# Gathers of a graph layer on GpSimd: a wait per gather for its own row buffer, and gather indices copied two tiles earlier

## What is computed

```python
def layer(h, params):
    W, b, g, beta = params
    h = h * norm_out
    agg = jax.ops.segment_sum(h[src], dst, num_segments=n)
    agg = agg * norm_in
    out = agg @ W + b
    out = _layer_norm(out, g, beta)
    out = jax.nn.gelu(out, approximate=False)
    return (out, None)
h, _ = jax.lax.scan(layer, features, (Ws, bs, ln_g, ln_b))
...
x = _layernorm(x + h)
```

## Time and profile before

| what | value |
|---|---|
| median of three runs | 1668.79 us (1665.58 to 1670.16) |
| profiled execution, its own time | 1669.91 us |
| its span, first to last instruction | 1668.2 us |
| mean granted TensorE clock | 0.808 of full speed |
| busy share of the span | TensorE 67%, weight loads 55%, DVE 53%, GpSimd 51%, ACT 32% |
| DMA | 224.52 MB moved, 135 GB/s |

### The profile page before, as it was taken

One profiled execution on the slowest core, in us unless ns is written; L12 is line 12 of the kernel. 1 busy time (PEld: TensorE's weight loads), 2 busy tenths in 40 slices (PEclk: granted clock), 3 DMA queues, 4 the chain that ended last, 5 costly groups with the idle time before them and its releaser, 6 DMA issues.

```text
span 1668.2 us, 29286 instructions
## 1 busy us (share of the span) xinstructions
PE 1110.4 (67%) x6235; PEld 916.9 (55%) x6235; DVE 880.2 (53%) x2153; ACT 528.1 (32%) x853; POOL 846.9 (51%) x1023
## 2 busy tenths in 40 slices
PE   7665378677596695776776696679956769992000
PEld 7444123666575575656656585667846667882000
DVE  6445577245354372463563274326733226776776
ACT  4132230232332332233333232333323333441444
POOL 1554300545445464455455365445745445765886
PEclk9556559788898897798898898789987889996555
DMA  0930000523514415225225324441244448545998
GB/s 14 377 130 3 2 1 6 159 82 126 158 57 139 133 69 170 78 107 163 71 106 164 107 76 138 139 126 66 91 139 147 149 126 321 189 169 180 312 302 291
DMA packets 98038, 224.52 MB, mean 135 GB/s; under 512 B 14496, under 2 KB 14496, under 8 KB 97968
## 3 DMA queue, kind: packets, MB, share of 16 engines
q0 software_dynamic: 34432, 104.72, 21.2%
q1 hardware_dynamic: 57200, 107.52, 17.9%
q10 hardware_dynamic: 6336, 11.54, 1.9%
HBM read 137.91 MB, written 85.82 MB: 134 GB/s over the span
## 4 chain that ended last, share of the span: by engine, by line
PE 53%; issue 12%; DMA 10%; DVE 8%; POOL 5%; ACT 4%; another core or an unknown queue 3%; ACTq 2%; DVEq 2%; POOLq 0%; SPq 0%
PE ps_a L1200 16%; PE ps_y L1220 9%; PE ps_y L1221 9%; PE ps_y L1225 9%; DMA rows<-h_rows,slot 4%; POOL rows L507 3%; DMA rows<-h_rows,idx_f 2%; PE ps_y L1216 2%; DMA h_rows<-rows 2%; PE ps_a L1115 2%; DVE agg_t L607 2%; PE ps_a L1181 1%; ACT agg_t L958 1%; DVEq L821 1%
## 5 line engine op out<-in xcount | busy, mean ns | idle before, releaser
L1200 PE MATMUL ps_a<-sel,rows 128*128 128x128 f32 x2560 | 407.0, 323 | 278.1 <-DVE sel L789 122.8
L1200 PEld LDWEIGHTS ps_a<-sel,rows 128*128 128x128 f32 x2560 | 377.1, 233 | 309.6 <-issue 309.0
L456 POOL DMA_INDIRECT rows<-h_rows,slot x290 | 279.8, 965 | 258.3 <-issue 124.6
L995 ACT ACTIVATE agg_t<-ps_a 128x508 f32 x320 | 190.7, 596 | 520.7 <-PE ps_a L1200 369.8
L464 POOL TENSOR_TENSOR s_lo<-agg_t,s_hi 128x512 fp32r<-128x512 f32 x168 | 216.9, 1293 | 251.3 <-ACT s_hi L1000 251.3
L789 DVE TENSOR_SCALAR sel<-iota,by_tile 128x128 f32<-128x128 f32 x344 | 126.0, 370 | 395.6 <-PE ps_a L1200 207.2
L1220 PE MATMUL ps_y<-w_hi,s_hi 128*128 128x512 f32 x672 | 268.5, 400 | 10.9 <-ACT s_hi L1000 10.8
L1221 PE MATMUL ps_y<-w_lo,s_hi 128*128 128x512 f32 x672 | 267.6, 398 | 0.0
L1225 PE MATMUL ps_y<-w_hi,s_lo 128*128 128x512 f32 x672 | 183.5, 396 | 0.0
L862 DVE BATCH_NORM_STATS2 small<-ps_y 128x6 f32<-128x512 f32 x168 | 117.3, 698 | 96.1 <-PE ps_y L1225 95.9
L1220 PEld LDWEIGHTS ps_y<-w_hi,s_hi 128*128 128x128 f32 x672 | 129.0, 192 | 42.0 <-issue 15.1
(11 more groups left out here) (210 smaller groups left out, 1268.2 us busy)
## 6 DMA issues: line engine op xcount, KB each, us to landing
h_rows<-rows SPq DMA_DIRECT2D x124, 256.0 KB, 2.0
h_rows<-agg_t SPq DMA_DIRECT2D x1, 20480.0 KB
out<-agg_t SPq DMA_DIRECT2D x78, 256.0 KB
agg_t<-in_x SPq DMA_DIRECT2D x19, 1024.0 KB, 5.7
h_rows<-rows ACTq DMA_DIRECT2D x44, 256.0 KB, 2.3
w_raw<-in_Ws SPq DMA_DIRECT2D x32, 256.0 KB
rows<-h_rows,slot POOLq DMA_INDIRECT x290
rows<-in_ln_g SPq DMA_DIRECT2D x8, 256.0 KB, 3.8
```

The source lines that it names most:

```text
L456: g.indirect_dma_start(out=rows[:, k, :], out_offset=None, in_=table[:, :], in_offset=bass.IndirectOffsetOnAxis(ap=slot[:, k:k + 1], axis=0))\
L995: a.activation(agg_t[:, :, bass.ds(r0 + 1, P - 1)], ps_a[k % GS][:, :, 1:P], ACT.Copy)\
L1200: m = mm(ps_a[k % GS][:, b, :], rows[:, k, b * P:(b + 1) * P], sel[:, k % GS, :], start=True, stop=True)
```

## The change

GpSimd now waits before every gather, for the tile that used this very row buffer ten tiles before. DVE copies a half's next indices at its third tile (k = 2 and 7) instead of its fifth (k = 4 and 9), and before that waits until the half's last gather of this group (k = 4 and 9) has landed, since this gather reads `slot` too. PRIME goes from 8 to 10, because the new wait reaches nine tiles back.

```diff
-PRIME = 8
+PRIME = 10
...
                         if k % GS == 0:
                             pool.wait_ge(ix_ok, ib * 2 + group * 2 + (L * 2 + k // GS + 1))
                             pool.sem_inc(tick, 1)
-                            pool.wait_ge(agg_ok, done(i + k - GS))
-                            pool.sem_inc(tick, 1)
+                        pool.wait_ge(agg_ok, done(i + k - UN + 1))
+                        pool.sem_inc(tick, 1)
                         g.indirect_dma_start(out=rows[:, k, :], out_offset=None, in_=table[:, :],
...
                             v.tensor_tensor(col, ps_a[k % GS][:, :, 0:1], col, ALU.add).then_inc(edge_ok, 1)
-                            if k % GS == GS - 1:
+                            if k % GS == GS - 3:
+                                dve.wait_ge(g_in[k + 2], (ib + group + 1) * 16)
                                 indices(L, t + k // GS * GS + UN, k // GS)
```

## The result

The changed kernel takes 1677.87 us, median of 8 runs (1672.67 to 1686.53), against 1667.9 for the kernel before in 8 runs of the same comparison. The ratio is 1.0067 with a 95% interval of 1.0038 to 1.0096: slower, by 11 us, where 1658 was forecast.

The account below looks back on a forecast made before the run. The prediction took late DVE selects, with late sums and index copies behind them, as the bound. Half of 25 us of gather waits, 12 us, with other terms at nothing, came off 1669.9 us to give 1658; range 1630 to 1702.

Parts of the forecast that it names:

- What bounds it: Sum-stage matmuls: TensorE idles mostly for DVE's select (122.8 us in layers two to eight), while late sums delay the index copy.
- the wait per gather: GpSimd's queue: 256 extra wait-and-tick pairs cost nothing, being worked off under the 0.95 us of the gather before.
- My upper bound of 77 us: GpSimd: without cover, each of the 256 extra pairs costs at most 0.30 us, 77 us of GpSimd time.
- The copy two tiles earlier: DVE's index copy at tiles 2 and 7: a burst of gathers may start 2.6 us sooner in its group.
- 12 of 25: Matmuls at L1200: half of the about 25 us of gather waits inside the stages is won, 12 us.
- The wait for gather 4 or 9: DVE, before its index copy, waits for this gather to land: cost 0, bound 0.6 us at 46 places, 28 us.
- a sign of being wrong altogether: DVE's copy idling for a gather, or gathers themselves growing longer than 0.95 us, would show the forecast wrong altogether.
- Gather waits: L1200's waits for gathers inside a layer, 25 us, should be near zero in the profile after.
- the second case: Cycle keeps its period, late tile moved by two, select waits growing as gather waits vanish: about 1669 us; chance 0.26.
- The slower rival: Layer starts: thirteen gathers in a row hold tile 3 back 3.75 us in 8 layers, 30 us: about 1700; chance 0.31.
- GpSimd as the bound: Sum stages freed from late notices run at the gathers' 1.25 us per tile, gaining 72 us: about 1600; chance 0.08.
- Contention with casts: Gathers beside DVE's weight casts take 1.24 instead of 0.95 us: 16 places, 5 us of GpSimd time at most.

Follow-up runs that it names:

- e_copy: Kernel before with only the early copy (tiles 2 and 7), one wait per half, PRIME 8; 1651.35 us, 0.9895, in a session with late notices.
- h_after: The changed kernel run again in a session without late notices, against the kernel before at 1517.57 us; 1514.51 us, 0.9979.
- g_copy: The early copy alone, one wait per half, run again in a session without late notices, against the kernel before at 1521.97 us; 0.9967.
- f_after: The changed kernel run again in a session with late notices, against the kernel before at 1668.99 us; 1680.22 us, 1.0055.

## Why the prediction was wrong

**What bounds it** held: selects that come late, with the copy behind them, and not the gathers.

**The step that failed is the wait per gather, costed at nothing.** Its own reason was right: 256 pairs are worked off under the gathers, which keep 0.30 us between them. But the increments lengthen somebody else's wait. With them, the release of TensorE's notice in the midst of a burst goes missing (tile 2 at 14.18 instead of 10.95 us). At the layers' starts alone this is 212.6 - 206.0 = 6.6 us, of the 11 us measured. Alone the increments gave 1.0064, waits and increments 1.0054 and 1.0084: 9 to 14 us. In the traces TensorE's waits for select grow: 150.0 us with the increments, 139.2 and 135.2 with the waits, 122.8 before. My upper bound of 77 us covered the size, but for GpSimd's time, which did not grow.

**The copy two tiles earlier** was right in sign and by its path, and half as large again as forecast: 18 us gained alone (14 to 22 by the interval) where I took 12 of 25, with 23 us of gather waits gone and the select waits level. In the changed kernel that gain is not there, and this is the other half of the miss. The trace says why so far as it can: the copy now hangs on tiles 2 and 7, and these are the ones whose early release goes missing. At the third layer's start the copy stands 15.3 us after the first gather in the changed kernel and 11.3 us with the copy alone; in the last layer six of nine releases (five in the second profile) come 2.2 us or more behind the burst, and none with the copy alone. That this is the whole of the interaction was not shown: the kernel that would, copy and increments together, only met sessions without late notices.

**The wait for gather 4 or 9, costed at 0**, is near enough. No copy behind a layer's first tile idles over 0.2 us in after. In `e_copy` five of 64 do, 3.8 us together, all over 10 us after their gather's issue, and the trace names no gather for them. Where notices are on time DVE does idle for the gather before a few copies: three in `h_after`, 1.6 us together, and two in `g_copy`, 2.1 us. I had called that a sign of being wrong altogether, which it is not at this size.

**Gather waits.** Those inside a layer did vanish as forecast, and the select waits grew by the same 21 us. That was my sign for the second case, the cycle that keeps its period with its late tile moved by two, and so far it came true: the late tiles moved from the fifth to the third of a half, and 119.0 us in the last layer became 123.8 in one profile and 119.7 in the other. What the case missed are the layers' starts. In this pair of profiles the idle time at the matmuls stayed level and their busy time grew by 12.8 us, with a granted clock of 0.797 against 0.808. That difference is not the change's: in 13 further runs of the kernel before the clock was 0.795 to 0.804, in the 8 of the changed one 0.794 to 0.804. In the other profile of the changed kernel, `f_after`, the matmuls were busy 412.3 us and idle 278.5.

**The slower rival** gave 1700 by a mechanism that did not happen. It wanted thirteen gathers in a row, so that tile 3 would be held behind them; it took from the earlier trace rows that tile 2 gets through before the ten are out. With late notices there are ten in a row and a pause (535.89 to 540.97), since with the waits tile 2, too, is held until the ten are out. Where notices are on time the next half does follow the ten at once (`h_after`), and tile 3 is not held. Its forecast that the notice follows the last issue by over 2 us was the sound part.

**GpSimd as the bound, about 1600 at 0.08**: sessions without late notices show what it was about, 65 gathers in 89.5 us or 6.9 us per five, and 1514 us. But it is not the change that does it: there the kernel before is at 1518 to 1522 as well. Nor is DVE held to the 1.3 us per tile that I took from the earlier trace rows: in `h_after` it sees tiles 3 to 7 of the third layer 0.97 or 0.98 us apart.

**Contention with casts** at 5 us or less is neither confirmed nor contradicted; the gathers' busy sum is 277.7 us in 290 issues, 958 ns each, against 279.8 us and 965 ns before. Nothing like 4 us more for one gather stands in the traces: the longest gather of the sum stages took 1.24 us before and 1.19 us after.

The early copy alone beats the kernel before in both kinds of session: 0.9895 where notices are late, 0.9967 where they are not. Against the changed kernel it is ahead only where they are late; where they are not, 0.9967 and 0.9979 can't be told apart.

## What to carry to other kernels

Here the added waits and increments were free for their own queue and not for the kernel. Where a signal of another engine is seen late while a queue issues DMAs, ask what each added semaphore instruction in that queue does to the signal, and measure the waits alone, apart from the reordering they are meant to allow. And time a kernel with such stalls in more than one session: here the same edit is 0.6% slower in one kind and perhaps 0.2% faster in the other.

## What the hardware showed that I had not expected

- TensorE's increments of `agg_ok` are seen late by DVE and ACT alike, 5 us late where DVE idled 5.74 us for tile 2, while GpSimd issues indirect gathers. In the first profile of the changed kernel the release at a layer's start comes 2.5 to 2.9 us after the burst's last issue and brings three tiles' notices at once; with a quarter of the bytes notices are still late (tile 3 at 14.0 us or more); with copies in the gathers' place they are on time (1501 instead of 1669 us).
- The kernel before took 1668 to 1669 us in the first comparison and two sessions more, and 1518 to 1522 in three others, each time with all of its runs within 1% of the median. Most of the difference stands in the sum stages, where the notices are late: with late notices they take some 59 us for 30 tiles, without them some 48. In the traces of the sessions at 1518 to 1522 no select came over 1.5 us after both its tile's last matmul and DVE's work before; with late notices it is up to 5.7 us. It is not simply the chip: the record gives the same chip number, 9, to the session at 1522.01 and to the one at 1668.99. What sets a session apart I don't know.
- The traces differ in one more thing. The gathers of the eight layers raise their semaphores 5120 times; the traces without late notices hold 5104 to 5121 records of it, those with late notices 2017 to 2738. The data move on all the same: in the third layer of the changed kernel 52 to 76 DMA packets start in each us from 5 to 14 us after the first gather, and 51 to 70 in `h_after`. So raises that engines wait for are late just where records of raises are missing. Whether the recording itself takes part was not tested: every run on record has its span and clock taken.
- Why a semaphore increment between two gathers, which GpSimd works off many gathers ahead of the issue that the trace shows, takes away a release in the midst of the burst stays open. The changed kernel without the increments, with its waits put on the gathers themselves, was not tried.
